# A selective scan's driving product on VectorE, and attention scores stored negated and scaled with the exponential's bias taken from their minimum

## The chip, the core and the metric

The program runs on one core of a Trainium2 chip. The core has five engines with instruction queues of their own: TensorE (PE in the rows, with PEld for its weight loads), VectorE (DVE), ScalarE (ACT), GpSimd (POOL) and SyncE (SP), which here only issues DMA transfers. Each queue runs in order, and semaphores tie the queues together. The metric is the device time of one execution in microseconds; less is better.

## What is computed

The input is x (4 sequences of 256 tokens, width 256) and a context ctx (4 x 256 x 128). Four layers add to x one after the other; each normalises x first, and the attention's queries, both mixtures' inputs and the scan's gate read the normalised x.

```
x = x + ssm(ctx, layernorm(x))          # scan over 256 steps, 16 states, 256 channels
x = x + moe0(layernorm(x))              # 32 experts of width 96, top 8
x = x + attention(layernorm(x), ctx)    # 16 heads, 8 key/value heads, head size 128
x = x + moe1(layernorm(x))              # 16 experts of width 128, top 2, and a shared one
```

The two places that the change touches compute this:

```
state = state * exp(d_t * A) + (d_t * u_t) * B_t       # for each of 16 states
y_t   = sum over states of state * C_t
scores = q @ k.T / sqrt(128);  attn = softmax(scores)
```

## The kernel before, in words

The 1024 tokens are worked on in two halves (h = 0, 1) of 512 tokens, with channels or features on the 128 partitions. Matrix products of the mixtures and of attention are made from pairs of rounded parts: `product3` (L86 to L88) issues three matmuls for one product, and each operand exists as a high part, which ScalarE rounds (L660), and a rest, which VectorE subtracts (L915; L1373 on GpSimd for weights, w_lo from w_raw and w_hi).

**The scan.** For half h and state n, index i = 16 h + n. ScalarE makes decay_t = exp(delta * A) (L700, a ring of five). GpSimd makes the driving product drive = delta_u * B_n (L1363, `make_drive`, two buffers), where B_n is one row of 512 values that a DMA spreads over all partitions (b_rows, three buffers). VectorE runs the recurrence over 1024 elements per partition in one instruction (L1001, `scan_state`), and multiplies the state by C_n, which comes in c_rows likewise (L1019, `scan_read`). TensorE sums these products over the states with an identity (L370, y_sum). Every buffer is guarded by a semaphore: drive i waits for scan i-2, scan i for drive i and decay i, load_b(i) for drive i-3.

In half 0 the scan stands nearly alone: between its states VectorE also normalises z_gate (L946), and after state 7 makes softplus_floor for half 1 (L961), which waits for TensorE's dt product (L363). Then come the gate, the addition to x, the norm, and the first router (L1064 to L1087, move_route at L1135). In half 1 the scan is woven into the units of the first mixture. A unit u is 128 hidden features for 512 tokens: gate_up (12 matmuls) and down (6 matmuls) on TensorE, ScalarE's SiLU (L770) and rounding, and on VectorE two hidden products (L1173, and L1176 with the routing weights), the rest hidden_lo (L915), one scan_state and one scan_read. Every other unit also adds two read_outs (L1027, `add_pair`). The order is written out by hand in each engine's block. GpSimd makes one w_lo per unit besides the drive products. The queue of SyncE issues in this order: the load of b_rows(1, 3), the store of the routes, c_rows(1, 3), b_rows(1, 4), and then the route_bc loads of the first units.

**The attention.** 64 head units, four to a group. For unit i TensorE makes scores in PSUM. VectorE's `mask_scores` (L1287) adds the mask, writes scores_sb, and takes the maximum of each row in the same instruction (once for each of two row blocks, with a small second instruction that writes out row_max). Then it makes row_bias = -SCALE * row_max (L1291), two values per partition. ScalarE's `soften` (L866) makes exp(SCALE * scores + row_bias) with its sum. VectorE inverts the sum (L1279), GpSimd multiplies (L1432, L1435), TensorE turns the probabilities (L576), ScalarE rounds them, and VectorE makes probs_t_lo (L915), for unit i-2, right behind row_bias of unit i. turn_probs on TensorE waits for probs_t_lo of the unit before it, since both use bank 6.

## Time and profile before

| | us |
|---|---|
| median of 3 runs (876.93 to 877.42) | 877.03 |
| profiled execution, its own time | 877.58 |
| its span | 875.5 |
| PE busy | 729.7 (83%) |
| DVE busy | 649.3 (74%) |
| ACT busy | 434.7 (50%) |
| POOL busy | 397.1 (45%) |
| L1363 drive products, 32 on POOL | 101.4, mean 3.174 |
| L1001 scans, 32 on DVE | 103.6, mean 3.237 |
| b_rows load, issue to landing, median | 3.7 |

Shares of the span in the chain of work that ended last, by line: PE L86, L87 and L88 13% each, DVE state L1001 9%, DVE read_out L1019 4%, ACT probs L866 4%, DVE scores L1287 3%, DVE row_bias L1291 3%.

Times in the rows are in microseconds from the start of the span. A busy time contains what an instruction waited for inside the engine after its start. Matmuls overlap, so the distance of their starts tells more than their durations.

### The profile page before, as it was taken

To read this page: it belongs to the slowest core of one execution; us is meant where nothing else is said; L and a number is where in the kernel's file an instruction comes from. 1 tells how busy PE (TensorE), PEld (TensorE's weight loads), DVE (VectorE), ACT (ScalarE), POOL (GpSimd) and SP (SyncE) were. 2 spreads that over 40 slices of the span, in tenths; PEclk is the share of its full clock that TensorE was granted. 3 is DMA by queue.
4 is the path that set the end of the run, shared out by engine and by line. 5 is a ranking of instruction groups with operands and counts; after the bars stand their busy time and mean duration, and the time that the engine had idled before them with its cause. 6 is when DMAs were issued, how large, how long until landed. Compare 5 with 4: busy or idle time off the path is not lost.

```text
span 875.5 us, 10280 instructions
## 1 busy us (share of the span) xinstructions
PE 729.7 (83%) x3448; PEld 559.9 (64%) x3448; DVE 649.3 (74%) x1151; ACT 434.7 (50%) x836; POOL 397.1 (45%) x291
## 2 busy tenths in 40 slices
PE   4256553587687899999989999999899989999997
PEld 1012111455454678888778888887788876788886
DVE  6999988799999856655478778778677756554554
ACT  5443301556642344444456666765666645333342
POOL 0455554477775324445354554544345533222131
PEclk8576665789999999999989999999999999899999
DMA  5223230255445325444110111110012123333340
GB/s 185 70 94 89 84 120 19 75 163 161 155 135 153 122 72 172 153 161 151 61 60 32 40 53 31 49 43 31 19 45 67 49 73 127 128 117 105 103 127 24
DMA packets 40531, 81.33 MB, mean 93 GB/s; under 512 B 5752, under 2 KB 8064, under 8 KB 40480
## 3 DMA queue, kind: packets, MB, share of 16 engines
q1 hardware_dynamic: 40480, 80.69, 29.3%
q8 instruction: 27, 0.44, 0.2%
q14 instruction: 24, 0.20, 0.1%
HBM read 79.30 MB, written 1.38 MB: 92 GB/s over the span
## 4 chain that ended last, share of the span: by engine, by line
PE 43%; DVE 33%; issue 12%; ACT 9%; POOL 1%; DMA 1%; SPq 0%; DVEq 0%; ACTq 0%; POOLq 0%
PE bank L86 13%; PE bank L87 13%; PE bank L88 13%; DVE state L1001 9%; DVE read_out L1019 4%; ACT probs L866 4%; DVE scores L1287 3%; DVE row_bias L1291 3%; PE bank L576 2%; DVE bank L1173 1%; ACT q_t_hi L660 1%; DVE u_sb L926 1%; DVE x_norm L946 1%; ACT w_hi L660 1%; DVE probs_t_lo L915 1%
## 5 line engine op out<-in xcount | busy, mean ns | idle before, releaser
L1373 POOL TENSOR_TENSOR w_lo<-w_raw,w_hi 128x768 fp32r<-128x768 f32 (+1 forms) x106 | 201.3, 1899 | 247.0 <-ACT w_hi L660 246.7
L86 PE MATMUL bank<-xt_hi,w_hi 128*128 128x512 f32 x400 | 167.1, 418 | 15.8 <-DVE hidden_lo L915 15.8
L660 ACT ACTIVATE w_hi<-w_raw 128x768 fp32r<-128x768 f32 (+1 forms) x106 | 85.7, 811 | 161.1 <-PE bank L88 125.0
L87 PE MATMUL bank<-xt_lo,w_hi 128*128 128x512 f32 x400 | 159.8, 399 | 0.0
L88 PE MATMUL bank<-xt_hi,w_lo 128*128 128x512 f32 x400 | 159.7, 399 | 0.0
L370 PE MATMUL bank<-read_out,identity 128*128 128x512 f32 x96 | 69.4, 863 | 71.6 <-DVE read_out L1019 57.3
L1363 POOL TENSOR_TENSOR drive<-delta_u,b_rows 128x1024 f32<-128x1024 f32 x32 | 101.4, 3174 | 37.0 <-DVE state L1001 36.3
L660 ACT ACTIVATE hidden_hi<-bank 128x512 fp32r<-128x512 f32 x84 | 49.4, 588 | 109.8 <-DVE bank L1176 108.3
L1001 DVE TENSOR_TENSOR_SCAN state<-decay_t,drive 128x1024 f32<-128x1024 f32 x32 | 103.6, 3237 | 0.0
L86 PEld LDWEIGHTS bank<-xt_hi,w_hi 128*128 128x128 f32 x400 | 76.7, 192 | 38.3 <-DVE hidden_lo L915 19.1
L915 DVE TENSOR_TENSOR hidden_lo<-bank,hidden_hi 128x512 fp32r<-128x512 f32 x84 | 57.5, 684 | 58.2 <-ACT hidden_hi L660 58.1
L370 PEld LDWEIGHTS bank<-read_out,identity 128*128 128x128 f32 x96 | 21.8, 250 | 113.1 <-DVE read_out L1019 74.3
L1173 DVE TENSOR_TENSOR bank<-gated,bank 128x512 f32<-128x512 f32 x80 | 55.4, 692 | 51.1 <-PE bank L88 49.9
L866 ACT ACTIVATE probs<-scores,row_bias 128x256 f32<-128x256 f32 x128 | 63.8, 500 | 53.8 <-DVE row_bias L1291 53.5
L87 PEld LDWEIGHTS bank<-xt_lo,w_hi 128*128 128x128 f32 x400 | 76.8, 192 | 18.7 <-issue 2.7
L88 PEld LDWEIGHTS bank<-xt_hi,w_lo 128*128 128x128 f32 x400 | 76.2, 190 | 18.7
L1435 POOL TENSOR_TENSOR probs<-probs,row_scale 128x512 f32<-128x512 f32 x64 | 66.6, 1040 | 5.0
L86 PE MATMUL bank<-hidden_hi,w_hi 128*128 128x512 f32 x168 | 66.9, 398 | 1.1 <-DVE hidden_lo L915 1.1
L87 PE MATMUL bank<-hidden_lo,w_hi 128*128 128x512 f32 x168 | 66.9, 398 | 0.0
L88 PE MATMUL bank<-hidden_hi,w_lo 128*128 128x512 f32 x168 | 66.3, 395 | 0.0
L1432 POOL TENSOR_TENSOR row_scale<-row_scale,any_valid 128x2 f32<-128x2 f32 x64 | 12.5, 195 | 111.3 <-DVE row_scale L1279 111.3
L1176 DVE TENSOR_TENSOR bank<-bank,route_bc 128x512 f32<-128x512 f32 x80 | 55.9, 699 | 7.6 <-DMA route_bc<-route_scratch 4.9
(172 smaller groups left out, 1562.9 us busy)
## 6 DMA issues: line engine op xcount, KB each, us to landing
...
```

Of the source, the lines that this page charges most:

```text
L86: e.matmul(out, w_hi, m_hi, start=first, stop=False)
L87: e.matmul(out, w_hi, m_lo, start=False, stop=False)
L88: return e.matmul(out, w_lo, m_hi, start=False, stop=last)
L370: last = e.matmul(ps[:, :], identity[:, :], tile[:, c, :], start=first, stop=n == DS - 1)
L660: e.activation(out, source, ACT.Copy).then_inc(sem(name), 1)
L866: last = e.activation(probs[i % 3][:, r, :], scores_sb[i % 2][:, r, :], ACT.Exp, scale=SCALE, bias=row_bias[i % 2][:, r:r + 1], accum_out= ...
L915: e.tensor_tensor(out_lo, source, out_hi.bitcast(F32), ALU.subtract).then_inc(sem(name), 1)
L1001: e.tensor_tensor_scan(flat2(state[i % 2][:, :, :]), flat2(decay_t[i % 5][:, :, :]), flat2(drive[i % 2][:, :, :]), 0.0, ALU.mult, ALU.add) ...
L1173: e.tensor_tensor(h, g, h, ALU.mult).then_inc(sem("mul"), 1)
L1363: e.tensor_tensor(drive[i % 2][:, :, :], delta_u[:, h, :, :], b_rows[i % 3][:, :].unsqueeze(1).broadcast_to([P, EH, HT]), ALU.mult).then_i ...
L1373: e.tensor_tensor(lo[:, 0:n], w_raw[p % RAW][:, 0:n], hi[:, 0:n].bitcast(F32), ALU.subtract).then_inc(sem("w_lo"), 1)
L1435: e.tensor_tensor(probs[i % 3][:, :, :], probs[i % 3][:, :, :], row_scale[i % 3][:, :].unsqueeze(2).broadcast_to([P, 2, SEQ]), ALU.mult).t ...
```

## The change

Two edits. The function `make_drive` leaves GpSimd's block; as `scan_drive` it stands in VectorE's block, with the same waits and the same operands. VectorE issues drive(h, 0) ahead of the first scan of a half, and drive(h, n + 1) right behind scan (h, n), ahead of its scan_read (in half 1 also ahead of hidden_lo). GpSimd keeps the weight remainders, the small powers and the attention's products.

In the attention, the two score instructions now compute (score + mask) * -SCALE and take the minimum of a row. ScalarE's exponential has scale -1 and takes that minimum as its bias, so L1291 and the buffers row_max and row_bias are gone, and `soften` waits for the score instructions themselves.

```diff
         v_split = [split_pair(f"v{i}", [P, HC, HD]) for i in range(2)]
         q_split = [split_pair(f"q_t{i}", [P, HT]) for i in range(4)]
         scores_sb = [place(f"scores{i}", [P, 2, SEQ]) for i in range(2)]
-        row_max = [place(f"row_max{i}", [P, 2]) for i in range(2)]
-        row_bias = [place(f"row_bias{i}", [P, 2]) for i in range(2)]
+        row_min = [place(f"row_min{i}", [P, 2]) for i in range(2)]
         probs = [place(f"probs{i}", [P, 2, SEQ]) for i in range(3)]
         row_sum = [place(f"row_sum{i}", [P, 2]) for i in range(3)]
         row_scale = [place(f"row_scale{i}", [P, 2]) for i in range(3)]
...
                     copy(head_out[j % 2][0][:, :], bank[7][:, :], "head_hi")

             def soften(i):
-                at.wait_ge("row_bias", i + 1)
+                at.wait_ge("masked", 2 * i + 2)
                 at.wait_ge("probs_turn", i - 2)
                 for r in range(2):
-                    last = e.activation(probs[i % 3][:, r, :], scores_sb[i % 2][:, r, :], ACT.Exp, scale=SCALE,
-                                        bias=row_bias[i % 2][:, r:r + 1], accum_out=row_sum[i % 3][:, r:r + 1])
+                    last = e.activation(probs[i % 3][:, r, :], scores_sb[i % 2][:, r, :], ACT.Exp, scale=-1.0,
+                                        bias=row_min[i % 2][:, r:r + 1], accum_out=row_sum[i % 3][:, r:r + 1])
                 last.then_inc(sem("exp"), 1)

             copy_acc(5)
...
                     e.tensor_copy(hi[:, :, :], raw[:, :, :]).then_inc(sem("gates_split"), 1)
                     at.wait_ge("gates_split", 2 * i + 1)
                     split_rest(lo[:, :, :], raw[:, :, :], hi[:, :, :], "gates_split")
+
+            def scan_drive(h, n):
+                if n >= DS:
+                    return
+                i = h * DS + n
+                at.wait_ge("conv", 2 * HALVES)
+                at.wait_ge(f"delta_u{h}", EH)
+                at.wait_ge(f"ld_b{i % 3}", 16 * (i // 3 + 1))
+                at.wait_ge("state", i - 1)
+                e.tensor_tensor(drive[i % 2][:, :, :], delta_u[:, h, :, :],
+                                b_rows[i % 3][:, :].unsqueeze(1).broadcast_to([P, EH, HT]),
+                                ALU.mult).then_inc(sem("drive"), 1)

             def scan_state(h, n):
                 i = h * DS + n
...
             softplus_excess(0)
             make_delta(0)
             split_gates()
+            scan_drive(0, 0)
             for n in range(DS):
                 scan_state(0, n)
+                scan_drive(0, n + 1)
                 scan_read(0, n)
                 if n == 0:
                     at.wait_ge("ld_x1", 16)
...
             make_delta(1)
             choose_eight(2)
             move_route(2)
+            scan_drive(1, 0)
             scan_state(1, 0)
+            scan_drive(1, 1)
             scan_read(1, 0)


...
                     add_pair(n - 1)
                 if n < DS:
                     scan_state(1, n)
+                    scan_drive(1, n + 1)
                 if FFN0_CHUNKS + 1 <= u <= FFN0_CHUNKS + 7:
                     transition(4, u - FFN0_CHUNKS - 1)
                 if u == U0 - 8:
...
                 at.wait_ge("exp", i - 1)
                 for r in range(2):
                     e.tensor_tensor_reduce(scores_sb[i % 2][:, r, :], bank[4 + i % 2][:, r * SEQ:(r + 1) * SEQ],
-                                           mask_bias[:, half * HB + b, :], 1.0, -3.0e38, ALU.add, ALU.max,
-                                           row_max[i % 2][:, r:r + 1]).then_inc(sem("masked"), 1)
-                at.wait_ge("masked", 2 * i + 2)
-                e.tensor_scalar(row_bias[i % 2][:, :], row_max[i % 2][:, :], -SCALE, None,
-                                ALU.mult).then_inc(sem("row_bias"), 1)
+                                           mask_bias[:, half * HB + b, :], -SCALE, 3.0e38, ALU.add, ALU.min,
+                                           row_min[i % 2][:, r:r + 1]).then_inc(sem("masked"), 1)

             def rest_probs(i):
                 hi, lo = probs_t[i % 2]
...
                 at.wait_ge("var", count)
                 e.tensor_tensor(rstd[h][:, :], rstd[h][:, :], half_power[:, :], ALU.pow).then_inc(sem("rstd"), 1)

-            def make_drive(h, n):
-                i = h * DS + n
-                at.wait_ge("conv", 2 * HALVES)
-                at.wait_ge(f"delta_u{h}", EH)
-                at.wait_ge(f"ld_b{i % 3}", 16 * (i // 3 + 1))
-                at.wait_ge("state", i - 1)
-                e.tensor_tensor(drive[i % 2][:, :, :], delta_u[:, h, :, :],
-                                b_rows[i % 3][:, :].unsqueeze(1).broadcast_to([P, EH, HT]),
-                                ALU.mult).then_inc(sem("drive"), 1)
-
             def rest_weights(p):
                 if p >= PIECES:
                     return
...
                     at.wait_ge("delta", EH)
                 e.memset(decay_t[i][:, :, :].rearrange("p c (b s) -> p (c b) s", b=HB)[:, :, 0:1],
                          0.0).then_inc(sem("decay_pad"), 1)
-            make_drive(0, 0)
-            for n in range(DS):
-                if n + 1 < DS:
-                    make_drive(0, n + 1)
-                if n == 0:
-                    scale_norm(1, 2)
+            scale_norm(1, 2)
             rest_weights(0)
             rest_weights(1)
             scale_norm(0, 3)
...
                 at.wait_ge("u", 2 + c + 1)
                 e.tensor_tensor(delta_u[:, 1, c, :], delta[:, 1, c, :], u_sb[:, 1, c, :],
                                 ALU.mult).then_inc(sem("delta_u1"), 1)
-            make_drive(1, 0)
-            make_drive(1, 1)


             for u in range(U0):
...
                     at.wait_ge("ctx_hi", 1)
                     e.tensor_tensor(ctx_lo[:, :], ctx_sb[:, :], ctx_hi[:, :].bitcast(F32),
                                     ALU.subtract).then_inc(sem("ctx_split"), 1)
-                if n + 1 < DS:
-                    make_drive(1, n + 1)
                 if n == DS + 2:
                     scale_norm(1, 4)

```

VectorE in half 0 around states 10 to 12, before:

```order
L1001 SCALAR_TENSOR_TENSOR state0_131<-decay_t0_122,drive0_133 128x1024 [waits read,drive,decay]
L1019 TENSOR_TENSOR read_out2_129<-state0_131,c_rows1_120 128x1024 [waits y_sum0,ld_c1,state]
L1001 SCALAR_TENSOR_TENSOR state1_132<-decay_t1_123,drive1_134 128x1024 [waits read,drive,decay]
L1019 TENSOR_TENSOR read_out3_130<-state1_132,c_rows2_121 128x1024 [waits y_sum0,ld_c2,state]
L1001 SCALAR_TENSOR_TENSOR state0_131<-decay_t2_124,drive0_133 128x1024 [waits read,drive,decay]
```

and after, where a drive product stands behind each scan, and waits for nothing but its b_rows:

```order
L1012 SCALAR_TENSOR_TENSOR state0_131<-decay_t0_122,drive0_133 128x1024 [waits read,drive,decay]
L1003 TENSOR_TENSOR drive1_134<-delta_u_113,b_rows2_118 128x1024 [waits ld_b2]
L1030 TENSOR_TENSOR read_out2_129<-state0_131,c_rows1_120 128x1024 [waits y_sum0,ld_c1,state]
L1012 SCALAR_TENSOR_TENSOR state1_132<-decay_t1_123,drive1_134 128x1024 [waits read,drive,decay]
L1003 TENSOR_TENSOR drive0_133<-delta_u_113,b_rows0_116 128x1024 [waits ld_b0]
L1030 TENSOR_TENSOR read_out3_130<-state1_132,c_rows2_121 128x1024 [waits y_sum0,ld_c2,state]
L1012 SCALAR_TENSOR_TENSOR state0_131<-decay_t2_124,drive0_133 128x1024 [waits read,drive,decay]
```

What moved: between two scans stood one product, now there are two.

GpSimd from the last states of half 0 on, before:

```order
L1363 TENSOR_TENSOR drive0_133<-delta_u_113,b_rows2_118 128x1024 [waits state,ld_b2]
L1363 TENSOR_TENSOR drive1_134<-delta_u_113,b_rows0_116 128x1024 [waits state,ld_b0]
L1373 TENSOR_TENSOR w0_lo_92<-w_raw0_88,w0_hi_91 128x768 [waits w_hi]
L1373 TENSOR_TENSOR w1_lo_94<-w_raw1_89,w1_hi_93 128x768 [waits w_hi]
L1355 TENSOR_TENSOR rstd0_72<-rstd0_72,half_power_65 128x4 [waits var]
L1373 TENSOR_TENSOR w4_lo_136<-w_raw2_90,w4_hi_135 128x768 [waits w_hi]
```

and after, from the small fills at its beginning on:

```order
L1392 MEMSET decay_t4_126 128x4 [waits delta]
L1368 TENSOR_TENSOR rstd1_73<-rstd1_73,half_power_65 128x4 [waits var]
L1376 TENSOR_TENSOR w0_lo_92<-w_raw0_88,w0_hi_91 128x768 [waits w_hi]
L1376 TENSOR_TENSOR w1_lo_94<-w_raw1_89,w1_hi_93 128x768 [waits w_hi]
L1368 TENSOR_TENSOR rstd0_72<-rstd0_72,half_power_65 128x4 [waits var]
```

What moved: the remainders of the first two weight pieces (w0_lo, w1_lo) have no drive product ahead of them any more, only the power for rstd1.

VectorE in half 1, two units without and with a pair sum (from the second hidden product of the first on; bank5, then bank7), before:

```order
L1176 TENSOR_TENSOR bank5<-bank5,route_bc2_109 128x512 [waits ld_route2,mul]
L1001 SCALAR_TENSOR_TENSOR state1_132<-decay_t4_126,drive1_134 128x1024 [waits drive,decay]
L915 TENSOR_TENSOR hidden2_lo_106<-bank5,hidden2_hi_105 128x512 [waits hid_hi]
L1019 TENSOR_TENSOR read_out0_127<-state1_132,c_rows1_120 128x1024 [waits ld_c1,state]
L1173 TENSOR_TENSOR bank7<-gated1_100,bank7 128x512 [waits up,silu]
L1176 TENSOR_TENSOR bank7<-bank7,route_bc3_110 128x512 [waits ld_route3,mul]
L1027 TENSOR_TENSOR read_out0_127<-read_out0_127,read_out3_130 128x1024 [waits read]
L1001 SCALAR_TENSOR_TENSOR state0_131<-decay_t0_122,drive0_133 128x1024 [waits drive,decay]
L915 TENSOR_TENSOR hidden0_lo_102<-bank7,hidden0_hi_101 128x512 [waits hid_hi]
L1019 TENSOR_TENSOR read_out1_128<-state0_131,c_rows2_121 128x1024 [waits pair,ld_c2,state]
```

and after:

```order
L1187 TENSOR_TENSOR bank5<-bank5,route_bc2_109 128x512 [waits ld_route2,mul]
L1012 SCALAR_TENSOR_TENSOR state1_132<-decay_t4_126,drive1_134 128x1024 [waits drive,decay]
L1003 TENSOR_TENSOR drive0_133<-delta_u_113,b_rows2_118 128x1024 [waits ld_b2]
L914 TENSOR_TENSOR hidden2_lo_106<-bank5,hidden2_hi_105 128x512 [waits hid_hi]
L1030 TENSOR_TENSOR read_out0_127<-state1_132,c_rows1_120 128x1024 [waits ld_c1,state]
L1184 TENSOR_TENSOR bank7<-gated1_100,bank7 128x512 [waits up,silu]
L1187 TENSOR_TENSOR bank7<-bank7,route_bc3_110 128x512 [waits ld_route3,mul]
L1038 TENSOR_TENSOR read_out0_127<-read_out0_127,read_out3_130 128x1024 [waits read]
L1012 SCALAR_TENSOR_TENSOR state0_131<-decay_t0_122,drive0_133 128x1024 [waits drive,decay]
L1003 TENSOR_TENSOR drive1_134<-delta_u_113,b_rows0_116 128x1024 [waits ld_b0]
L914 TENSOR_TENSOR hidden0_lo_102<-bank7,hidden0_hi_101 128x512 [waits hid_hi]
L1030 TENSOR_TENSOR read_out1_128<-state0_131,c_rows2_121 128x1024 [waits pair,ld_c2,state]
```

What moved: behind each scan stands a drive product, ahead of hidden_lo, for which TensorE waits.

## Rows read from the trace of the kernel before

**Rows 1.** Busy time of each engine by stretch: us, then busy of PE, PEld, DVE, ACT, POOL, PEclk.

```profile
202.73:218.05 15.32, 12.29 (x40) 7.96 (x40) 15.25 (x13) 8.86 (x13) 11.85 (x5) 0.89 0.50 151
172.75:177.45 4.70, 4.70 (x12) 3.31 (x10) 4.67 (x4) 4.13 (x6) 3.71 (x2) 0.50 0.33 119
640.00:665.00 25.00, 24.78 (x169) 22.25 (x168) 19.75 (x58) 17.59 (x45) 13.03 (x17) 1.00 0.16 54
```

**Rows 2.** Timeline, half 0, one state: start, us, engine, line, operation, what, idle before.

```profile
67.85 1.22 DVE L1019 TENSOR_TENSOR read_out<-state,c_rows 128x1024 f32<-128x1024 f32 x1
67.96 3.32 POOL L1363 TENSOR_TENSOR drive<-delta_u,b_rows 128x1024 f32<-128x1024 f32 x1 [2.29 <-DVE state L1001]
68.99 4.43 DVE L1001 TENSOR_TENSOR_SCAN state<-decay_t,drive 128x1024 f32<-128x1024 f32 x1
...
73.46 1.23 DVE L1019 TENSOR_TENSOR read_out<-state,c_rows 128x1024 f32<-128x1024 f32 x1
```

**Rows 3.** Timeline of VectorE, start of the scan.

```profile
28.62 2.33 DVE L992 CAST cent_hi<-cent_raw 128x32 fp32r<-128x32 f32 x1
...
33.19 2.28 DVE L1001 TENSOR_TENSOR_SCAN state<-decay_t,drive 128x1024 f32<-128x1024 f32 x1
...
42.05 6.72 DVE L946 TENSOR_SCALAR z_gate<-x_tok,mean_var,rstd 128x256 f32<-128x256 f32 x8
48.69 2.28 DVE L1001 TENSOR_TENSOR_SCAN state<-decay_t,drive 128x1024 f32<-128x1024 f32 x1
```

**Rows 4.** Timeline, half 0, the scan behind softplus_floor.

```profile
83.05 2.28 DVE L1001 TENSOR_TENSOR_SCAN state<-decay_t,drive 128x1024 f32<-128x1024 f32 x1
```

**Rows 5.** Timeline of VectorE, end of half 0's scan.

```profile
119.05 2.64 DVE L1019 TENSOR_TENSOR read_out<-state,c_rows 128x1024 f32<-128x1024 f32 x1
...
121.61 3.89 DVE L1001 TENSOR_TENSOR_SCAN state<-decay_t,drive 128x1024 f32<-128x1024 f32 x1
...
125.53 1.23 DVE L1019 TENSOR_TENSOR read_out<-state,c_rows 128x1024 f32<-128x1024 f32 x1
```

**Rows 6.** Timeline of VectorE, router and first unit.

```profile
152.16 1.86 DVE L1075 TENSOR_TENSOR route_a<-logits,top 128x128 f32<-128x128 f32 x1
...
153.95 2.42 DVE L1077 TENSOR_TENSOR route_a<-route_a,top 128x128 f32<-128x128 f32 x1
...
168.63 0.70 DVE L1176 TENSOR_TENSOR bank<-bank,route_bc 128x512 f32<-128x512 f32 x1 [4.28 <-DMA route_bc<-route_scratch]
```

**Rows 7.** Timeline, half 1, a unit with a pair sum and one without; then GpSimd.

```profile
190.22 0.70 DVE L1176 TENSOR_TENSOR bank<-bank,route_bc 128x512 f32<-128x512 f32 x1
190.83 2.07 DVE L1027 TENSOR_TENSOR read_out<-read_out,read_out 128x1024 f32<-128x1024 f32 x1
192.82 2.28 DVE L1001 TENSOR_TENSOR_SCAN state<-decay_t,drive 128x1024 f32<-128x1024 f32 x1
...
195.60 2.22 DVE L1019 TENSOR_TENSOR read_out<-state,c_rows 128x1024 f32<-128x1024 f32 x1
...
199.07 3.16 DVE L1001 TENSOR_TENSOR_SCAN state<-decay_t,drive 128x1024 f32<-128x1024 f32 x1
...
194.27 2.47 POOL L1373 TENSOR_TENSOR w_lo<-w_raw,w_hi 128x768 fp32r<-128x768 f32 x1 [2.46 <-ACT w_hi L660]
...
201.08 2.78 POOL L1373 TENSOR_TENSOR w_lo<-w_raw,w_hi 128x768 fp32r<-128x768 f32 x1 [1.01 <-ACT w_hi L660]
```

**Rows 8.** Attention: all L1291; timeline of POOL, DVE and PE; then TensorE's wait in total.

```profile
L1291 DVE TENSOR_SCALAR row_bias<-row_max x64: 169/708/772, 436.4 to 697.5; 128x2 f32<-128x2 f32 x64
...
526.40 1.04 POOL L1435 TENSOR_TENSOR probs<-probs,row_scale 128x512 f32<-128x512 f32 x1
...
527.38 0.68 DVE L915 TENSOR_TENSOR probs_t_lo<-bank,probs_t_hi 128x512 fp32r<-128x512 f32 x1
...
528.21 0.63 PE L576 MATMUL bank<-identity,probs 128*128 128x128 f32 x4 [0.27 <-DVE probs_t_lo L915]
...
PE bank L576 <- DVE probs_t_lo L915: 10.5, 18, 2.7
```

## The prediction

> **What bounds the kernel now.** I read the busy times by stretch first [rows 1]. In two units of the second half's scan (202.73 to 218.05) VectorE is busy 15.25 of 15.32 us, TensorE 12.29; in the attention stretch 640 to 665 us TensorE is busy 24.8 of 25.0 us. So there are two regimes, and the two edits fall one in each. The chain of waits, read after that, names the same lines (table of the section on the profile): state L1001 and read_out L1019, scores L1287 and row_bias L1291 beside the matmuls.
>
> Then the timeline of VectorE and GpSimd over one state of the first half [rows 2]. The reader is to see two things. The scan takes 4.43 us when GpSimd's drive product lies over it, but 2.28 us alone (48.69 in [rows 3]). And GpSimd's product, issued at 67.96 while the read_out product (67.85, 1.22 us) runs, ends at 71.28; the scan, issued at 68.99, ends at 73.42, which is 2.14 us after that. The two never work at once: VectorE's operations with two SBUF inputs and GpSimd's products take turns. GpSimd held the turn from 69.07 to 71.28, 2.2 us. It was waiting and got it at the end of the read_out product, ahead of a scan that VectorE had issued already. One state costs 1.14 + 2.2 + 2.2 = 5.6 us, the distance of 67.85 and 73.46. VectorE looks busy throughout, and 2.2 us of each state are GpSimd's.
>
> The Trainium skill, "SBUF — State Buffer", section "SBUF: two separate sides", describes this as an exclusive lock between VectorE and GpSimd that the first starter holds for a whole instruction, while the loser blocks fully. The rows agree on the lock; on who wins they show the waiting GpSimd served before a VectorE instruction issued back to back. [...]
>
> **Drive product, first half.** On VectorE it is the same shape and form as the read_out product: 1.22 us, 1.14 us from start to start. A state becomes 2.20 (scan) + 1.14 (drive) + 1.14 (read_out) = 4.48 us. From the start: delta_u is done at 28.3 us in both. Before, two small casts of the centroids wait for GpSimd (28.62, 2.33 us and so on) and the first scan starts at 33.19 [rows 3]. After, they take some 0.2 us each, the drive follows (1.2 us), and scan 0 starts at 30.3. From scan 0 to scan 2 it was 15.5 us (33.19 to 48.69), 6.72 of them eight z_gate normalisations with two GpSimd products over them. Less two turns of 2.2 us they leave 2.3; I take 2.6, as the first turn had begun before them. The other 8.8 us stay, and two drives of 1.14 come to them: 13.7 us. Scan 2 starts at 44.0 instead of 48.69. To scan 15 there are 13 states: 58.2 us, 102.2.
>
> Three additions. The two softplus_floor instructions cost 1.4 us. They also wait for the dt matmuls, which follow the y_sum that starts when read_out 6 is done (74.69): scan 8 came at 83.05 [rows 4], 8.36 us after it, and with 4.48 us states VectorE would be there 2.5 us sooner. TensorE does not get faster, so I keep that 2.5 us (0 if its clock is higher there, since those matmuls ran at the lower level). Third, the weight remainders w_lo 0 and 1 stood in GpSimd's queue behind all drive products; now they run as soon as ScalarE has rounded the weights, inside the scan. They cost about what they cost before [rows 5]: read_out took 2.64 us instead of 1.22 and the scan 3.89 instead of 2.28. I take 2 x 1.6 = 3.2 us. Sum: 102.2 + 1.4 + 2.5 + 3.2 = 109.3 for scan 15, and 2.3 later read_out 15, 111.6, against 125.53. I take **a gain of 14.0 us** (12 to 16.5).
>
> **Between the halves.** Two drive products of GpSimd block two tiny routing subtractions: from 152.16 to 156.37 [rows 6], which would take 0.6 us. That is 3.6 us gained. But drive(1,0) now stands on VectorE behind move_route, drive(1,1) ahead of read_out(1,0), so read_out(1,0) ends 2.3 us later relative to move_route. The queue of SyncE issues c_rows after that read_out, and the broadcast routes behind c_rows; the first hidden product waits for them until 168.63. The route store waits behind a b_rows load for drive(1,0), 1.1 us, which that leaves covered. **Gain 1.3 us** (-1 to 3.6). What is late next is the same route load.
>
> **Drive product, second half.** Here the change loses. [rows 7] show a unit pair. Two hidden products and hidden_lo have one input in PSUM and are never stretched: GpSimd's 2.2 us turn lay mostly under them. Per pair VectorE was stretched by 0.84 (read_out sum, 2.07 us instead of 1.23), 0.99 (read_out, 2.22), 0.89 (scan, 3.16) and 0.97 (the other read_out), 3.7 us of 15.36. Without that the pair needs 11.66; two drives make it 13.94. What is left of GpSimd is one w_lo per unit, a turn of 1.63 us (194.27 + 2.47 less the end of the scan at 195.10, and likewise in each pair). In the unit without a pair sum it is asked for 1.9 us after the second hidden product, in the middle of the scan (201.08). So GpSimd gets its turn at the scan's end, and what stands next is now the drive, not hidden_lo: 1.6 us blocked. In the pair unit ScalarE loads a table first and w_lo is asked for at 3.35 us (194.27). Without stretching, the pair sum and scan end 3.33 us after the hidden product. I take it that the drive gets through first, and that hidden_lo then covers 0.6 us: 1.0 us blocked. A pair takes 13.94 + 1.6 + 1.0 = 16.54 us, 1.2 more than before. Six full pairs give 7.2. The first unit gives 1.8 (1.14 + 1.6 - 0.97), and the last pair, with one drive, gives back 0.6. **Loss 8.4 us** (bounds: 13 lost if every w_lo meets a drive; 12 gained if w_lo hid under the two hidden products, 0.3 left of it). I take the value nearest to the measured request times.
>
> Each load of b_rows now waits for a VectorE product, one state later than before, but has three states (13 us or more) to land in; the loads land in 3.7 us in the median (table). What hides this is gone only if a load took over 13 us.
>
> **Row bias.** The 64 instructions have a median of 0.71 us [rows 8] for two elements per row, the minimum being 0.17: the probs product of GpSimd (526.40, 1.04 us) lies over them. The Trainium skill, "VectorE: DVE Perf Modes", section "The TRN2 errata — SBUF-src ops pay a fixed extra latency per instruction", counts 58 cycles fixed cost, 0.06 us, for such an instruction; by that the edit would be worth an estimated 4 us of VectorE time, by the row 45 us. The row decides, but VectorE is not the bound here. The scale and the minimum ride in the same two score instructions, whose length I leave; ScalarE's exponentials start some 0.7 us earlier, into slack.
>
> What reaches the end is TensorE's wait for probs_t_lo, which stands right behind row_bias on VectorE: 18 waits, 10.5 us [rows 8]. Moving it 0.62 us forward removes the shorter ones whole and 0.62 of each longer one (five are longer): 6.7 us. In steady attention such a wait stands once in four units; the one at 528.21, 0.27 us, is of that kind. Two waits for the probs of GpSimd and one for x_tok, each longer than 0.62 us and behind the same instruction, come to it: 1.8 us. **Gain 8.5 us** (4 to 12). Next late is TensorE's own stream.
>
> **Sum.** 14.0 + 1.3 - 8.4 + 8.5 = 15.4 us. The profiled execution took 877.58 us, of which 2.1 lie outside its span of 875.5; it stands 0.55 us above the median of the three runs, 877.03. From its own time the sum gives 862.2, from the median 861.6: I forecast 861.6 us, its own range 857.5 to 865.
>
> **The rivals.**
> A. VectorE keeps its turn through back-to-back instructions, and w_lo starts under hidden_lo in every unit. Blocked 1.0 in place of 1.6 in seven units, 4.2 us: 857.4; with later requests that fall under the hidden products, down to 851. Against it: the scan issued at 68.99 that lost to GpSimd. For it: nothing shows this with a w_lo and a drive. Chance 0.13.
> B. w_lo also cuts in ahead of the drive in pair units, since 3.33 and 3.35 us are a toss: 0.6 x 7 = 4.2 us more, 865.8. Chance 0.2.
> C. The attention edit gains nothing, as TensorE then waits as long for another (ScalarE's rounding, GpSimd's probs). For it: TensorE is busy 99% of 640 to 665 us. Against it: each of the 18 waits is named. 870.1. Chance 0.12.
> D. Slower. VectorE's longer second half thins TensorE's work until its clock stays at the lower of its two levels (1.2 GHz). At that level the matmuls start 0.43 us apart (11 starts in 4.70 us, and the tail of one more, at a granted clock of 0.50, [rows 1]), so a unit's 18 matmuls and its share of y_sum take 18 x 0.43 + 1.9 = 9.6 us (the y_sum's 1.9 is half of the four records of a pair, 3.8 us at this level). Units would be 9.6 us in place of 7.68; 15 of them lose 28.8 us where the rest gains 23.8: 882.0. It decides from 13 such units of the 15 on (12.4 x 1.92 = 23.8). Against it: the granted clock is 0.89 in a pair [rows 1] and would have to fall throughout; a slow TensorE is also a busier one. Chance 0.03.
> E. The change doesn't do what it says: the drive on VectorE still takes turns with GpSimd for its whole length, because weight remainders fill GpSimd's free time in the first half as well. But the order of GpSimd has only two of them there. Otherwise the first half would keep its 5.6 us states and gain only the 4.7 us before scan 2: 870.8. Chance 0.04.
>
> **Chances.** Forecast 0.48, B 0.2, A 0.13, C 0.12, D 0.03, E 0.04. The range 854 to 871 reaches over the forecast, B, C, E and most of A. Out stay D, the lower end of A (0.04) and pairs of cases that add up beyond an end (A with the wait for dt gone, B with C), some 0.1: 0.17 in all. A measurement of this kernel tells 0.2% (1.8 us) from no change. Faster by more: 0.95; within: 0.02; slower: 0.03.
>
> **What would show it.** First half: scans of 2.28 us every 4.48 us, scan 0 at 30.3, read_out 15 near 111.6, and two places with w_lo. Second half: pairs of 16.5 us, drives of 2.8 us in one unit and 1.2 in the next. Attention: no L1291, four units 0.3 to 0.4 us shorter than before, the wait of TensorE for probs_t_lo under 4 us. I am wrong if the second half's pairs are not longer than 15.36 us, or if the attention's units keep their length.

## The result, and the profile after

The changed kernel takes 853.2 us (median of four runs, 851.77 to 855.85) against 877.14 us of the kernel before: ratio 0.973 (0.9706 to 0.9755), 24 us faster. Forecast was 861.6, and the range began at 854.0. The profiled execution is the slowest of the four, 855.85 us with a span of 853.9; against the 877.58 us of the profile before it gains 21.7. The forecast started from a median of three runs before, 877.03; with a fourth it is 877.14.

The page after, engines and the scan's line (busy in us, mean ns of one; idle before):

```profile
PE 728.4 (85%) x3448; PEld 566.6 (66%) x3448; DVE 600.3 (70%) x1119; ACT 435.3 (51%) x836; POOL 292.6 (34%) x259
...
L1012 DVE TENSOR_TENSOR_SCAN state<-decay_t,drive 128x1024 f32<-128x1024 f32 x32 | 73.1, 2284 | 0.3 <-ACT decay_t L699 0.2
```

GpSimd lost 104.5 us of busy time. VectorE took over 32 products and is still 49 us less busy: its scans take 2.28 us, not 3.24, and row_bias is gone.

Half 0, the timeline of VectorE, one state (answers to [rows 2, 3]), and where w_lo 0 and 1 run (answers to [rows 5]); the last row is GpSimd's:

```profile
43.82 2.28 DVE L1012 TENSOR_TENSOR_SCAN state<-decay_t,drive 128x1024 f32<-128x1024 f32 x1
46.02 1.20 DVE L1003 TENSOR_TENSOR drive<-delta_u,b_rows 128x1024 f32<-128x1024 f32 x1
47.13 1.22 DVE L1030 TENSOR_TENSOR read_out<-state,c_rows 128x1024 f32<-128x1024 f32 x1
48.27 2.29 DVE L1012 TENSOR_TENSOR_SCAN state<-decay_t,drive 128x1024 f32<-128x1024 f32 x1
...
89.42 2.76 DVE L1003 TENSOR_TENSOR drive<-delta_u,b_rows 128x1024 f32<-128x1024 f32 x1
92.10 2.82 DVE L1030 TENSOR_TENSOR read_out<-state,c_rows 128x1024 f32<-128x1024 f32 x1
...
87.22 6.61 POOL L1376 TENSOR_TENSOR w_lo<-w_raw,w_hi 128x768 fp32r<-128x768 f32 x2 [47.35 <-ACT w_hi L659]
```

Half 1, the pair of units (answers to [rows 7]), VectorE and then GpSimd:

```profile
159.14 1.22 DVE L1038 TENSOR_TENSOR read_out<-read_out,read_out 128x1024 f32<-128x1024 f32 x1
...
162.47 1.20 DVE L1003 TENSOR_TENSOR drive<-delta_u,b_rows 128x1024 f32<-128x1024 f32 x1
...
164.19 2.26 DVE L1030 TENSOR_TENSOR read_out<-state,c_rows 128x1024 f32<-128x1024 f32 x1
...
167.70 2.28 DVE L1012 TENSOR_TENSOR_SCAN state<-decay_t,drive 128x1024 f32<-128x1024 f32 x1
169.89 2.76 DVE L1003 TENSOR_TENSOR drive<-delta_u,b_rows 128x1024 f32<-128x1024 f32 x1
...
175.64 1.22 DVE L1038 TENSOR_TENSOR read_out<-read_out,read_out 128x1024 f32<-128x1024 f32 x1
...
162.58 2.78 POOL L1376 TENSOR_TENSOR w_lo<-w_raw,w_hi 128x768 fp32r<-128x768 f32 x1 [7.50 <-ACT w_hi L659]
169.72 1.86 POOL L1376 TENSOR_TENSOR w_lo<-w_raw,w_hi 128x768 fp32r<-128x768 f32 x1 [4.35 <-ACT w_hi L659]
```

In the attention the waits view has no wait of TensorE for probs_t_lo any more (10.5 us in [rows 8]). First what TensorE waited for GpSimd's probs before; then, after the change, ScalarE's wait for the scores and TensorE's for GpSimd's probs (us in total, times, longest):

```profile
PE bank L576 <- POOL probs L1435: 3.4, 2, 2.2
```

```profile
ACT probs L865 <- DVE row_min L1303: 24.5, 22, 2.9
...
PE bank L575 <- POOL probs L1429: 6.1, 6, 2.1
```

Subtracting the start of the same instruction in both traces gives the gain along the run. The table has these gains in us for all kernels of the experiments, each from its own profile against the profile before; numbers count from 0, and in the attention the instruction is the first score matmul of the unit. "Attention" is the last column less the one ahead of it; it starts from unit 4 to leave out the first wait, whose length differs between executions. Each number comes from one execution. bias_only, which changes nothing ahead of the attention, shows 0.6 to 1.5 us there, and that is about how far such a gain can be trusted.

| kernel | scan 8 | scan 15 | first hidden_lo | hidden_lo 14 | attention unit 4 | unit 63 | attention | ratio (interval) |
|---|---|---|---|---|---|---|---|---|
| changed kernel | 9.2 | 13.4 | 15.4 | 8.4 | 8.5 | 21.6 | 13.1 | 0.973 (0.9706 to 0.9755) |
| bias_only | 1.5 | 0.6 | 1.0 | 1.0 | 1.1 | 14.5 | 13.4 | 0.9835 (0.9815 to 0.9855) |
| drive_only | 9.5 | 13.7 | 15.1 | 8.2 | 8.1 | 6.7 | -1.4 | 0.987 (0.985 to 0.989) |
| drive_half0 | 11.3 | 15.5 | 18.5 | 18.5 | 17.0 | 30.3 | 13.3 | 0.9642 (0.9623 to 0.9661) |
| timed_w_lo | 10.5 | 14.7 | 18.0 | 21.3 | 20.3 | 33.7 | 13.4 | 0.9612 (0.9595 to 0.9629) |
| small_w_lo | 9.3 | 13.6 | 15.1 | 24.4 | 25.5 | 38.6 | 13.1 | 0.9518 (0.9493 to 0.9543) |
| drive_behind_hidden | 11.3 | 15.5 | 19.8 | 13.8 | 13.9 | 27.0 | 13.1 | 0.9687 (0.9668 to 0.9707) |
| tiny_sbuf | 11.3 | 15.5 | 17.5 | 10.6 | 10.5 | 20.4 | 9.9 | 0.9772 (0.9748 to 0.9797) |
| tiny_psum | 11.2 | 15.4 | 17.4 | 10.5 | 10.5 | 23.4 | 12.9 | 0.9712 (0.9693 to 0.9731) |
| link_late | 10.0 | 14.2 | 16.0 | 9.1 | 8.2 | 8.0 | -0.2 | 0.9886 (0.986 to 0.9912) |
| timed_route | 11.4 | 15.6 | 22.4 | 25.7 | 26.3 | 40.6 | 14.3 | 0.9574 (0.9555 to 0.9594) |
| timed_route_late | 10.0 | 17.4 | 24.0 | 27.2 | 26.5 | 39.9 | 13.4 | 0.9526 (0.9507 to 0.9545) |

### The profile page after: what moved, and what is told of

Its sections match the earlier page's. It is cut to its first block, busy times and chain, and to the rows that moved or that the text cites. A ratio compares the mean times of both kernels' runs of the same rounds, so it can differ in the third digit from the quotient of the medians.

```text
span 853.9 us, 10187 instructions
## 1 busy us (share of the span) xinstructions
PE 728.4 (85%) x3448; PEld 566.6 (66%) x3448; DVE 600.3 (70%) x1119; ACT 435.3 (51%) x836; POOL 292.6 (34%) x259
## 4 chain that ended last, share of the span: by engine, by line
PE 56%; DVE 14%; issue 8%; ACT 4%; POOL 1%; DMA 0%; SPq 0%; DVEq 0%; ACTq 0%; POOLq 0%
PE bank L86 17%; PE bank L87 17%; PE bank L88 17%; PE bank L575 3%; DVE read_out L1030 3%; DVE state L1012 3%; DVE bank L1184 1%; DVE hidden_lo L914 1%; ACT probs L865 1%; DVE read_out L1038 1%; POOL probs L1429 1%; DVE bank L1187 1%; ACT w_hi L659 1%; PE bank L399 1%; DVE x_tok L1055 1%
## 5 line engine op out<-in xcount | busy, mean ns | idle before, releaser
L1376 POOL TENSOR_TENSOR w_lo<-w_raw,w_hi 128x768 fp32r<-128x768 f32 (+1 forms) x106 | 197.3, 1862 | 371.8 <-ACT w_hi L659 371.5
L86 PE MATMUL bank<-xt_hi,w_hi 128*128 128x512 f32 x400 | 169.2, 423 | 36.8 <-DVE hidden_lo L914 36.8
L87 PE MATMUL bank<-xt_lo,w_hi 128*128 128x512 f32 x400 | 162.7, 407 | 0.0
L88 PE MATMUL bank<-xt_hi,w_lo 128*128 128x512 f32 x400 | 162.6, 407 | 0.0
L369 PE MATMUL bank<-read_out,identity 128*128 128x512 f32 x96 | 64.0, 804 | 41.5 <-DVE read_out L1030 40.0
L88 PEld LDWEIGHTS bank<-xt_hi,w_lo 128*128 128x128 f32 x400 | 78.0, 195 | 19.3
L865 ACT ACTIVATE probs<-scores,row_min 128x256 f32<-128x256 f32 x128 | 63.6, 499 | 24.6 <-DVE row_min L1303 24.5
L369 PEld LDWEIGHTS bank<-read_out,identity 128*128 128x128 f32 x96 | 21.7, 244 | 80.0 <-DVE read_out L1030 58.4
L1012 DVE TENSOR_TENSOR_SCAN state<-decay_t,drive 128x1024 f32<-128x1024 f32 x32 | 73.1, 2284 | 0.3 <-ACT decay_t L699 0.2
L914 DVE TENSOR_TENSOR q_t_lo<-bank,q_t_hi 128x512 fp32r<-128x512 f32 x32 | 22.1, 692 | 58.3 <-ACT q_t_hi L659 58.3
L769 ACT ACTIVATE gated<-bank 128x512 f32<-128x512 f32 x84 | 50.2, 598 | 12.5 <-PE bank L88 12.1
```

Of the source, the lines that this page charges most:

```text
L86: e.matmul(out, w_hi, m_hi, start=first, stop=False)
L87: e.matmul(out, w_hi, m_lo, start=False, stop=False)
L88: return e.matmul(out, w_lo, m_hi, start=False, stop=last)
L369: last = e.matmul(ps[:, :], identity[:, :], tile[:, c, :], start=first, stop=n == DS - 1)
L865: last = e.activation(probs[i % 3][:, r, :], scores_sb[i % 2][:, r, :], ACT.Exp, scale=-1.0, bias=row_min[i % 2][:, r:r + 1], accum_out=ro ...
L914: e.tensor_tensor(out_lo, source, out_hi.bitcast(F32), ALU.subtract).then_inc(sem(name), 1)
```

## The experiments

### Each edit alone

bias_only is the kernel before with the four lines of the second edit; drive_only is the changed kernel with those four lines undone.

> The kernel before with the second edit alone (negated scores, their minimum as the bias); the driving products stay on GpSimd. Theory P, the record's sum: each wait of TensorE for probs_t_lo is shortened by at most 0.62 us, 8.5 us in all, 868.6 us. Theory Q: in the profiled run of after the gain grows from 8.4 us at the first scores to 21.6 us at the last, 13.2 us, since a wait that the view names with 0.27 us costs TensorE 0.57 us in the distance of its starts; then this edit alone gives 877.1 - 13.2 = 863.9 us. Theory R: part of what attention gained came from the other edit (TensorE's clock, another phase of GpSimd); then it lies between, or above 868.6.

> The changed kernel with the second edit undone (maximum and row_bias as before); the driving products on VectorE in both halves. The record's sum (14.0 + 1.3 - 8.4): 870.1 us. By the profile of after (15.0 for half 0, 3.0 between the halves, -9.6 for half 1): 877.1 - 8.4 = 868.7 us. If the edits add up, the gains of this kernel and of the bias alone sum to that of after, 24 us between the medians; if the edits help each other, they sum to less.

Measured: 863.0 us and 867.4 us, beside 877.9 of the kernel before on that chip. By the ratios the bias edit gains 14.5 us (12.7 to 16.2), 13.4 of it in the attention by the profile; theory Q holds and the record's 8.5 falls. The drive edit gains 11.4 us (9.7 to 13.2), where the prediction's sum had 6.9 and the profile after 8.4. Together that is 26, with the changed kernel at 24: within the intervals the edits add up. Theory R falls, as the attention gains 13.1 to 13.4 us in most kernels that have the bias edit as it is, wherever it stands in the run (14.3 in timed_route). The -1.4 of drive_only arises at one place, from 586 to 590 us, where its granted clock is at the lower level. In drive_only nearly all of the old wait is there:

```profile
PE bank L576 <- DVE probs_t_lo L915: 10.3, 17, 2.7
```

### Half 1: who pays for a turn

drive_half0 gives the products of half 1 back to GpSimd. In half 1's block of VectorE and of GpSimd:

```diff
-            scan_drive(1, 0)
             scan_state(1, 0)
-            scan_drive(1, 1)
...
                     scan_state(1, n)
-                    scan_drive(1, n + 1)
...
+            make_drive(1, 0)
+            make_drive(1, 1)
...
+                if n + 1 < DS:
+                    make_drive(1, n + 1)
```

> Both edits, but the driving products of half 1 are GpSimd's again, all 16 of them. Theory 1: VectorE's own work bounds the units of half 1, which cost 9.6 us (18.0 gained before them, 8.4 left behind them), with a pair of units at 16.50 us in place of 15.3. Without that: 853.2 - 9.6 = 843.6 us, less what the two routing subtractions and the first unit lose again (3.0 us at most): 843.6 to 846.6. Theory 2: the gain shrinks in half 1 for another reason (TensorE catches up, its clock, the route loads), and the units settle at the same distance whoever makes the product: 853 us.

Measured 847.1 us, 0.9642 (0.9623 to 0.9661), some 8 us under the changed kernel's ratio and 0.5 us above the end of theory 1's range. The gain stands at 18.5 us from the first unit to the last, so theory 1 holds in its mechanism: all of half 1's loss came from the product's place. Part was given back elsewhere: between units 19 and 20 the gain falls by 1.6. Columns as in [rows 1], drive_half0 and then the changed kernel at the same place of the program, TensorE having waited 2.6 us for x_norm in both:

```profile
283.00:286.00 3.00, 2.10 (x9) 2.06 (x10) 2.30 (x5) 0.79 (x2) 0.37 (x1) 0.66 0.84 256
286.00:289.00 3.00, 3.00 (x12) 2.34 (x11) 1.73 (x3) 1.76 (x4) 0.00 (x0) 0.77 0.41 112
```

```profile
293.00:296.00 3.00, 2.02 (x13) 1.84 (x14) 2.30 (x5) 0.70 (x2) 0.45 (x1) 1.00 0.86 247
```

The granted clock fell to the lower level there in the one and not in the other (0.66 and 0.77 against 1.00). In the profile of tiny_sbuf, which has half 1 as in the changed kernel, unit 20 is as late (5.69 us behind unit 19, where the changed kernel has 4.15), so this is no consequence of where the product stands.

small_w_lo, drive_behind_hidden and timed_w_lo leave the product on VectorE. Their edits, in this order:

```diff
-                e.tensor_tensor(lo[:, 0:n], w_raw[p % RAW][:, 0:n], hi[:, 0:n].bitcast(F32),
+                m = 2 if 6 <= p <= 18 else n
+                e.tensor_tensor(lo[:, 0:m], w_raw[p % RAW][:, 0:m], hi[:, 0:m].bitcast(F32),
...
                     scan_state(1, n)
-                    scan_drive(1, n + 1)
...
                 rest_hidden(u)
                 if n < DS:
+                    scan_drive(1, n + 1)
                     scan_read(1, n)
...
                 if u in split_in0:
+                    if u + 1 < DS:
+                        at.wait_ge("read", DS + u + 2)
                     rest_weights(split_in0[u])
```

> The changed kernel, where GpSimd makes only two of the 768 columns of each weight remainder for pieces 6 to 18 (asked for in units 3 to 15 of half 1); the rest of those remainders is left out. Theory 1, a unit of half 1 is VectorE's own time plus GpSimd's turns: a pair costs 13.94 us in place of 16.50; over units 3 to 15, 6.5 pairs, 16.6 us: 836.6 us, or 838.3 if TensorE's clock dips once behind the scan as it did with the drive on GpSimd. Theory 2, TensorE or its clock is next late right away: the pair stops falling at some 15 us, 843 us.

Measured 837.0 us. From the second pair on a pair takes 13.89 us; forecast 13.94. Turns are the only thing that VectorE's unit contains beside its own instructions, and TensorE is not next late at that length.

> The changed kernel, where the driving product of half 1's scan units stands behind hidden_lo, still ahead of read_out. Theory 1, the turn goes to GpSimd at the first change of instruction after it asks, and a product with an input in PSUM (hidden_lo, 0.60 us from start to start) works beside it: in the unit without a pair sum hidden_lo covers 0.6 of the 1.6 us; in the pair unit w_lo is asked for 0.1 us after hidden_lo starts, and the drive is blocked 1.1 us where read_out was blocked 1.04. A pair: 13.94 + 1.0 + 1.1 = 16.0 us, 0.46 less than 16.50, over 7 pairs 3.2 us: 850.0 us. Theory 2, GpSimd gets its turn only between two products that want it: no difference in the sum, 853 us.

Measured 850.9 us. A pair takes 16.1 us, 16.0 forecast, in place of 16.5. The trace shows both covers, hidden_lo unstretched and the drive behind it blocked by 1.26 and 1.0 us:

```profile
176.19 0.67 DVE L914 TENSOR_TENSOR hidden_lo<-bank,hidden_hi 128x512 fp32r<-128x512 f32 x1
176.77 2.46 DVE L1003 TENSOR_TENSOR drive<-delta_u,b_rows 128x1024 f32<-128x1024 f32 x1
...
183.82 0.67 DVE L914 TENSOR_TENSOR hidden_lo<-bank,hidden_hi 128x512 fp32r<-128x512 f32 x1
184.40 2.20 DVE L1003 TENSOR_TENSOR drive<-delta_u,b_rows 128x1024 f32<-128x1024 f32 x1
```

> The changed kernel, where GpSimd starts each weight remainder of half 1's scan units only when VectorE has finished that unit's read_out, so that the remainder falls under the two hidden products, which have an input in PSUM. Theory 1, the turn-taking of products with both inputs in SBUF: of the 1.63 us turn 1.2 us are covered, a pair costs 13.94 + 0.8 = 14.7 us instead of 16.50, over 7 pairs 12.6 us: 840.6 us. Theory 2, the remainder slows VectorE's PSUM products as well: the pair stays near 16.5, 853 us. Theory 3: the later remainder makes TensorE wait for its weights: above 853 us.

Measured 844.3 us, 3.7 above the forecast; theory 1 by its mechanism, with a pair of 14.98 us where 14.7 stood. That makes 2.0 us of the miss in seven pairs. Another 1.5 is the same loss between units 19 and 20 as in drive_half0, at a lower granted clock. The two hidden products keep their 0.69 and 0.70 us, the instruction behind them is stretched by 0.55 us (GpSimd's row last):

```profile
163.41 0.70 DVE L1187 TENSOR_TENSOR bank<-bank,route_bc 128x512 f32<-128x512 f32 x1
164.02 2.83 DVE L1012 TENSOR_TENSOR_SCAN state<-decay_t,drive 128x1024 f32<-128x1024 f32 x1
...
170.95 1.77 DVE L1038 TENSOR_TENSOR read_out<-read_out,read_out 128x1024 f32<-128x1024 f32 x1
...
162.85 1.86 POOL L1376 TENSOR_TENSOR w_lo<-w_raw,w_hi 128x768 fp32r<-128x768 f32 x1 [29.29 <-DVE read_out L1030]
```

The two products cover 1.17 us of it (162.85 to 164.02) and 0.55 is left, a turn of 1.72 us, not 1.63.

### Attention: what did row_bias delay?

Before the change row_bias delayed two things: probs_t_lo behind it on VectorE, and the exponential that waited for it. tiny_sbuf and tiny_psum put a spare instruction ahead of probs_t_lo, for the first delay alone; in link_late the exponential waits for one behind it, for the second alone.

```diff
                 at.wait_ge("probs_t_hi", i + 1)
+                e.tensor_scalar(spare[:, :], any_valid[:, 0:2], 1.0, None, ALU.mult)
                 split_rest(flat2(lo[:, :, :]), bank[6][:, :], flat2(hi[:, :, :]), "probs_t_lo")
```

(tiny_psum has `bank[6][:, 0:2]` in place of `any_valid[:, 0:2]`), and in link_late

```diff
                     rest_probs(i - 2)
+                if i < HEAD_UNITS:
+                    e.tensor_scalar(spare[:, :], any_valid[:, 0:2], 1.0, None, ALU.mult).then_inc(sem("linked"), 1)
...
                 at.wait_ge("masked", 2 * i + 2)
+                at.wait_ge("linked", i + 1)
```

> The changed kernel with one more instruction on VectorE ahead of each probs_t_lo: it multiplies two values per partition by 1 from SBUF to SBUF into a buffer that nobody reads, so it is as small as row_bias was and stands where row_bias stood, but nothing waits for it. Theory 1: attention gained through VectorE's time ahead of probs_t_lo, and GpSimd's probs product stretches such an instruction to 0.7 us; then most of the 13.3 us come back: 863 to 866 us. Theory 2: attention gained because ScalarE's exponentials no longer wait for a link of their own in the chain (scores, row_bias, exponential); then the spare instruction costs little: 853 to 855 us.

> The same spare instruction at the same place, but its two values come from PSUM (the bank that probs_t_lo reads next). Theory 1, turn-taking with GpSimd only for instructions that work in SBUF alone: it takes its own 0.2 us, not 0.7. The steady group of four units had 0.62 us more on VectorE and lost 0.69 us; 0.2 us of delay lies inside the slack that is left (0.62 less 0.42, the distance of the named wait), so only the dozen longer waits come back with 0.2 us each: 854 to 857 us. Theory 2, any instruction of VectorE waits for GpSimd's product: 863 to 866 us like the other one.

> The changed kernel with a spare instruction of two values per partition on VectorE directly behind probs_t_lo, for which ScalarE's exponential waits. So the exponential starts about as late behind the scores as before the change (0.6 us of probs_t_lo and 0.2 us, where it was 0.82 us), but nothing is put ahead of probs_t_lo. Together with tiny_sbuf it splits what row_bias did in two: a delay ahead of probs_t_lo alone gave back 2 of 13.2 us. Theory 1, a ring of VectorE and ScalarE: a later exponential makes k_t_hi, v_hi and q_t_hi late, which stand behind it on ScalarE, their remainders late on VectorE, and so the next scores and the next probs_t_lo; then most of the rest comes back here, 8 to 12 us: 861 to 865 us. Theory 2, the link matters little by itself and the two delays only cost together: 854 to 857 us.

Measured: 857.4, 853.4 and 868.5 us. The groups of spare instructions (busy, mean ns) in tiny_sbuf, tiny_psum, link_late:

```profile
L1311 DVE TENSOR_SCALAR spare<-any_valid 128x2 f32<-128x2 f32 x62 | 47.2, 761 | 1.5 <-ACT probs_t_hi L660 1.4
```

```profile
L1311 DVE TENSOR_SCALAR spare<-bank 128x2 f32<-128x2 f32 x63 | 9.8, 155 | 2.1 <-ACT probs_t_hi L660 2.1
```

```profile
L1332 DVE TENSOR_SCALAR spare<-any_valid 128x2 f32<-128x2 f32 x63 | 15.3, 243 | 0.0
```

None of the three landed where it was forecast. tiny_sbuf lies between its two theories (863 to 866 and 853 to 855 us), tiny_psum 0.6 us under its range, and link_late 3.5 us above the range of theory 1.

With its source in PSUM the instruction is not held up by GpSimd (0.16 us against 0.76), and neither is it much in link_late, where it stands behind probs_t_lo (0.24 us with both ends in SBUF). So turn-taking is confirmed, and it reaches further than the prediction's "two SBUF inputs": this instruction, as row_bias before it, has one. But tiny_sbuf put 47 us back on VectorE, more than the 43 us that row_bias had taken, and gave back only 3.2 us of the 13.1. link_late put back 15 us of VectorE time and gave back all of it (13.3; by the ratios 13.7). So the saved VectorE time was not what counted most; the start of the exponential was. Worked out from the timelines of steady attention (units 16 to 19 of each, which repeat up to unit 32), in us, each column in the order of the units:

| kernel | first q_t_lo matmul to scores on VectorE | scores to exponential | a group of four |
|---|---|---|---|
| before | 1.45, 2.08, 1.82, 2.46 | 1.60, 1.53, 1.53, 1.92 | 15.71 |
| changed | 1.44, 2.07, 1.28, 1.39 | 1.61, 0.79, 1.05, 2.42 | 15.05 |
| tiny_sbuf | 1.45, 2.07, 1.27, 1.40 | 1.60, 0.80, 1.04, 2.44 | 15.19 |
| link_late | 1.80, 2.43, 2.37, 3.06 | 1.59, 1.60, 1.60, 1.60 | 15.55 |

It is a ring. ScalarE rounds k_t, v and q_t behind the exponential, VectorE makes their remainders, and the next scores stand behind these on VectorE. A later exponential makes the next scores late (1.82 and 2.46 us in place of 1.28 and 1.39, the last two units of the group), and probs_t_lo gets that delay and row_bias's own. Half of the ring before the change, then its counterpart after:

```profile
526.30 0.42 DVE L1287 CUSTOM_DVE_ANT_0 scores<-bank,mask_bias 128x256 f32<-128x256 f32 x1
...
526.76 0.71 DVE L1291 TENSOR_SCALAR row_bias<-row_max 128x2 f32<-128x2 f32 x1
...
527.50 0.51 ACT L866 ACTIVATE probs<-scores,row_bias 128x256 f32<-128x256 f32 x1 [0.98 <-DVE row_bias L1291]
...
528.50 0.57 ACT L660 ACTIVATE v_hi<-bank 128x512 fp32r<-128x512 f32 x1
...
529.11 0.69 DVE L915 TENSOR_TENSOR v_lo<-bank,v_hi 128x512 fp32r<-128x512 f32 x1 [0.45 <-ACT v_hi L660]
```

```profile
512.82 0.42 DVE L1303 CUSTOM_DVE_ANT_0 scores<-bank,mask_bias 128x256 f32<-128x256 f32 x1
...
513.53 0.50 ACT L865 ACTIVATE probs<-scores,row_min 128x256 f32<-128x256 f32 x1
...
514.51 0.58 ACT L659 ACTIVATE v_hi<-bank 128x512 fp32r<-128x512 f32 x1
...
515.13 0.69 DVE L914 TENSOR_TENSOR v_lo<-bank,v_hi 128x512 fp32r<-128x512 f32 x1 [0.69 <-ACT v_hi L659]
```

From the second score instruction to v_lo it took 2.81 us before and takes 2.31. In the steady groups the two delays nearly add up: 0.14 us in tiny_sbuf and 0.50 in link_late, of the 0.66 that a group gained. Over the whole attention they make more than the gain, 3.2 and 13.3 us against 13.1. Link_late's exponential also waits for probs_t_lo, which the kernel before did not ask for, so it is no exact copy, and how much of its 13.3 us is this wait isn't known.

### A version that beats both

> As timed_w_lo, and the queue of SyncE issues the route_bc loads of the first units ahead of c_rows(1,3) and b_rows(1,4). Theory 1: the first route load was issued at 144.82, after two loads that waited for read_out(1,0) until 143.98; the store's issue ends at 140.2 and a store takes 3.1 us, so the load can be issued near 143, 1.9 us sooner, and doesn't share the queues with 512 KB of rows: 2 to 3 us off 844.3, 841.3 to 842.3 us. Theory 2: VectorE's first units had slack behind that wait, or the late rows make a read_out wait in unit 2: 844 us.

> As timed_route, and GpSimd makes the first two weight remainders only when VectorE has finished half 0's last read_out, in place of between scans 11 and 12. Theory 1, taking turns: the 3.2 us that they stretched a drive and a read_out by go; they now lie over 4 us in which VectorE waits 2 us for TensorE and then has products with an input in PSUM, and stretch the gate product by up to 0.8 us: 2.4 to 3.2 us less than timed_route, some 839 us. Theory 2: the loads behind them (the raw buffers come free later) are late for the first units of TensorE: no gain or a loss.

The edit of timed_route in SyncE's block, and the one of timed_route_late in GpSimd's:

```diff
             load_b(1, 3)
             store_route(2)
+            load_routes(3, 1)
             load_c(1, 3)
...
             scale_norm(1, 2)
+            at.wait_ge("read", DS)
             rest_weights(0)
```

Measured 840.0 and 837.0 us, theory 1 in both, and each more than forecast (841.3 to 842.3 and some 839). The first route load is issued at 141.88, in timed_w_lo at 144.82, and the hidden product of the first unit waits 1.34 us for it, where it waits 4.96 there and 4.68 in the changed kernel. The first hidden_lo gains 4.4 us on timed_w_lo's, 0.9 of which were there at scan 15 already:

```profile
141.88 3.07 SPq L1458 DMA_DIRECT2D route_bc<-route_scratch  x6
...
145.12 0.70 DVE L1187 TENSOR_TENSOR bank<-bank,route_bc 128x512 f32<-128x512 f32 x1 [1.34 <-DMA route_bc<-route_scratch]
```

In timed_route_late both first remainders (from 107.81, 3.57 us) lie over VectorE's wait for TensorE and the instruction with a PSUM input behind it, and nothing is stretched:

```profile
106.50 1.23 DVE L1030 TENSOR_TENSOR read_out<-state,c_rows 128x1024 f32<-128x1024 f32 x1
109.81 1.41 DVE L1044 SCALAR_TENSOR_TENSOR read_out<-u_sb,small_sb,bank 128x512 f32<-128x512 f32 x2 [2.08 <-PE bank L369]
...
107.81 3.57 POOL L1376 TENSOR_TENSOR w_lo<-w_raw,w_hi 128x768 fp32r<-128x768 f32 x2 [68.01 <-DVE read_out L1030]
```

From scan 11 to scan 15 it gains 3.2 us on timed_route. At 0.9526 (0.9507 to 0.9545) it is the fastest that computes everything, 40.7 us under the kernel before.

## Why the prediction was wrong, step by step

The step that failed is the attention's term, 8.5 us where 13.2 were measured: what removing row_bias does to TensorE. It comes last below, in the order of the run.

- **First half, 14.0 forecast, 15.0 in the profile.** Scan 0 at 30.39 (30.3), scan 2 at 43.82 (44.0), states of 4.45 us (4.48), two places with w_lo at 1.56 and 1.60 us (1.6): right. Read_out 15 started at 110.51 (111.6). The difference is the wait for the dt matmuls behind read_out 6. I kept 2.5 us of it; it is 1.8 in this execution, as long in those of drive_only and small_w_lo, and none in tiny_psum's. The head of the program is the same in the changed kernel and in tiny_psum, and TensorE's dt matmuls took nearly twice as long in the one as in the other (changed kernel, then tiny_psum):

```profile
68.66 3.77 PE L362 MATMUL bank<-x_dbl,dt_proj_sb 8*128 8x512 f32 x4
...
71.48 0.75 DVE L960 TENSOR_SCALAR delta<-bank,small_sb 128x512 f32<-128x512 f32 x1 [0.87 <-ACT x_norm L678]
```

```profile
68.11 1.98 PE L363 MATMUL bank<-x_dbl,dt_proj_sb 8*128 8x512 f32 x4
...
70.52 1.41 DVE L961 TENSOR_SCALAR delta<-bank,small_sb 128x512 f32<-128x512 f32 x2
```

  The gain at scan 8 is 9.2 in the one and 11.2 in the other. A difference of that size would be most of the 2.65 us by which the profiled execution stands above the median; the other executions have no trace that would show it. From 68 to 72 us the granted clock was 0.50, the lower level, in the one and 1.00 in the other.
- **Between the halves, 1.3 forecast, 3.0 measured** (18.0 at 150.59, against 168.63 of [rows 6]). The two routing subtractions take 0.28 us each, and drive(1,0) stands where I put it. 1.5 us came from the wait for y_sum behind read_out 15 (2.13 us, 3.65 before), which I hadn't listed. It is TensorE's clock and not the edit. TensorE's last four y_sum matmuls, before and then after (columns as in [rows 1]), ran at a granted clock of 0.55 and 1.00, and bias_only, whose scan is the one of before, waits 2.08 us as well:

```profile
126.80:130.40 3.60, 3.55 (x4) 1.17 (x4) 0.00 (x0) 0.00 (x0) 0.00 (x0) 0.55 0.71 249
```

```profile
111.90:113.80 1.90, 1.90 (x5) 0.61 (x4) 0.00 (x0) 0.00 (x0) 0.00 (x0) 1.00 0.30 84
```

- **Second half, 8.4 forecast, 9.6 measured.** The pair took 16.50 us (16.54), drives 2.76 and 1.20 us (2.8 and 1.2), GpSimd served ahead of a drive that was issued back to back: 169.72 and 169.89. The six pairs cost 7.0 us (7.2) and the first unit 1.7 (1.8). The last pair lost 0.9 us where I let it give back 0.6: I had set it against a full pair of before, and before's last pair had no drive over its last pair sum either and took 14.45 us. Rivals A and B are both out by these lengths.
- **Attention, 8.5 forecast, 13.2 measured: the step that failed.** "Moving it 0.62 us forward removes the shorter ones whole and 0.62 of each longer one": this took the removed instruction as a delay of one neighbour, and the exponentials as starting earlier "into slack". It also stood in the ring, and link_late shows that the earlier exponential was worth most of the gain. So the waits for probs_t_lo went whole, all 10.5 us and the longest of 2.7 us with them, where the sum took 6.7. The waits for GpSimd's probs, which the sum let shrink, grew from 3.4 to 6.1 us.

  The sizes were read too low as well. All waits of TensorE that the view names in the attention fell from 16.6 to 8.3 us, so that a forecast of 8.5 would have fitted them, by luck, but its instructions start 13.2 us sooner. Around the wait of 0.27 us at 528.21 in [rows 8], before; then the same place after:

```profile
527.66 0.28 PE L88 MATMUL bank<-k_t_hi,q_t_lo 128*128 128x256 f32 x1
...
528.71 0.38 PE L86 MATMUL bank<-probs_t_hi,v_hi 128*128 128x256 f32 x1
```

```profile
514.77 0.28 PE L88 MATMUL bank<-k_t_hi,q_t_lo 128*128 128x256 f32 x1
514.90 0.60 PE L575 MATMUL bank<-identity,probs 128*128 128x128 f32 x4
515.25 0.36 PE L86 MATMUL bank<-probs_t_hi,v_hi 128*128 128x256 f32 x1
```

  The transposes start 0.55 us after the last matmul ahead of them, after the change 0.13, and need 0.50 us to the next start in place of 0.35: 0.57 us for a row that says 0.27. How the 4.9 us that no row names divide over the attention isn't known beyond this place. Rival C, no gain, is out.

By the profiles the misses are 1.0, 1.7, -1.2 and 4.7 us, 6.2 of 6.3 in all. Without the attention's miss the sum would have held, but in part by luck: the clock's 1.5 us between the halves stands against the last pair's. The rest to the median, some 2 us, is the size of the dt matmuls' clock. Rivals D and E are out as well: a pair's granted clock is 0.91 (159.14 to 175.64), and half 0 has its short states. (E's time adds up to 870.9, not 870.8.) The direction, the turn-taking, and the loss in half 1 stood.

The Trainium skill, "SBUF — State Buffer", section "SBUF: two separate sides", gives the lock to whoever starts first, for a whole instruction. The traces agree on the length: w_lo ended at 171.58 (169.72 and 1.86), the blocked drive at 172.65, 1.07 us later. On the order they agree too, if the recorded starts are compared, since w_lo's lies 0.17 us ahead of the drive's. VectorE's queue being full did not help it: what GpSimd has asked for during one of its instructions comes ahead of the next.

**What stays open.** Why the clock is at one level or the other at 68 and at 284 us in executions of like programs isn't settled, and how TensorE's 18 waits divide between the ring and the direct delay is known only roughly, from two kernels that together give back more than was gained. Whether the wait for y_sum is 3.65 us in other executions of the kernel before isn't known either.
